# Window attention with a pooled branch: out products in turns, full v spread by DMAs, later batches loaded in pieces

## What is computed

```python
qkv = jnp.einsum('nchw,oc->nohw', xw, qkv_w)            # xw: windows of the normalised x
pooled = _avg_pool5(qkv)
msq = jnp.concatenate([qkv, pooled], axis=1)
msq = msq.reshape(N, -1, 3 * DIM, ws * ws).transpose(0, 1, 3, 2)
q = jax.nn.relu(msq[..., :DIM])
k = jax.nn.relu(msq[..., DIM:2 * DIM])
v = msq[..., 2 * DIM:]
v = jnp.pad(v, ((0, 0), (0, 0), (0, 0), (0, 1)), constant_values=1.0)
kv = jnp.einsum('ngld,nglm->ngdm', k, v)
out = jnp.einsum('ngld,ngdm->nglm', q, kv)
out = out[..., :-1] / (out[..., -1:] + 1e-15)
...
y = jnp.einsum('nchw,oc->nohw', out, proj_w)
y = y * inv[None, :, None, None] + (bn_beta - bn_mean * inv)[None, :, None, None]
return x + y
```

## Time and profile before

| | |
|---|---|
| time, median of three runs | 924.52 us (922.64 to 924.81) |
| the profiled execution's own time | 923.39 us |
| its span | 921.6 us |
| TensorE matmul busy | 862.7 us (94%) |
| TensorE weight load busy | 724.5 us (79%) |
| VectorE busy | 768.1 us (83%) |
| ScalarE busy | 608.1 us (66%) |
| GpSimd busy | 455.0 us (49%) |
| masked pooled v, 576 passes | 224.9 us |
| masked full v, 384 passes | 191.9 us |
| DMA | 38.77 MB |

### The profile page before, as it was taken

How to read it: one execution, slowest core, us unless ns; L and a number is a source line. 1 busy time by engine, 2 the same in 40 slices (tenths; PEclk the granted TensorE clock), 3 DMA queues, 4 the chain that set the end, 5 groups by cost and what they waited for, 6 DMA issues and landing times.

```text
span 921.6 us, 64898 instructions
## 1 busy us (share of the span) xinstructions
PE 862.7 (94%) x29282; PEld 724.5 (79%) x29282; DVE 768.1 (83%) x1624; ACT 608.1 (66%) x1542; POOL 455.0 (49%) x967
## 2 busy tenths in 40 slices
PE   0699999999999999999999999999999999999997
PEld 0577888888888888888888888888888888888885
DVE  7368898998878898998787989999887878787876
ACT  0456767676666767676767676666767676767673
POOL 1544545555454545454545555454545454545550
PEclk9989999999999999999999999999999999999999
DMA  9910000000000000000000000000000000000000
GB/s 380 432 52 17 26 18 26 17 26 17 26 18 26 18 26 17 26 18 26 26 18 26 18 26 17 26 17 27 17 26 17 26 18 26 22 21 26 18 26 27
DMA packets 15893, 38.77 MB, mean 42 GB/s; under 512 B 1888, under 2 KB 14688, under 8 KB 15456
## 3 DMA queue, kind: packets, MB, share of 16 engines
q1 hardware_dynamic: 15840, 38.26, 10.7%
HBM read 19.38 MB, written 18.87 MB: 42 GB/s over the span
## 4 chain that ended last, share of the span: by engine, by line
PE 42%; ACT 39%; issue 14%; DVE 4%; POOL 1%; DMA 0%; ACTq 0%; DVEq 0%; POOLq 0%
ACT vm_pool L305 20%; ACT vm_full L305 15%; PE ps L536 14%; PE ps L564 10%; PE ps L552 9%; PE ps L553 4%; PE ps L636 4%; ACT k_pool L292 3%; DVE stats L377 1%; PE ps L579 1%; PE ps L546 1%; DVE kvc_full L444 1%; DMA x_all<-x 0%; ACT o_sb L332 0%; DVE kvc_pool L444 0%
## 5 line engine op out<-in xcount | busy, mean ns | idle before, releaser
L255 POOL TENSOR_TENSOR xn<-x_all,mean_t 128x384 f32<-128x384 f32 x96 | 79.3, 826 | 388.5 <-PE ps L553 370.0
L305 ACT ACTIVATE vm_pool<-ps,cst 128x256 f32<-128x256 f32 x576 | 224.9, 543 | 0.4 <-PE ps L546 0.4
L444 DVE TENSOR_TENSOR kvc_full<-ps,cst 128x864 f32<-128x864 f32 x192 | 193.2, 1048 | 7.5 <-PE ps L564 7.5
L444 DVE TENSOR_TENSOR kvc_pool<-ps,cst 128x864 f32<-128x864 f32 x192 | 193.2, 1048 | 0.4 <-PE ps L564 0.4
L305 ACT ACTIVATE vm_full<-ps,cst 128x384 f32<-128x384 f32 x384 | 191.9, 597 | 0.9 <-PE ps L536 0.9
L312 ACT ACTIVATE q_full<-ps 128x384 f32<-128x384 f32 x96 | 47.1, 491 | 202.7 <-PE ps L552 202.7
L536 PE MATMUL ps<-wkv_sb,xn 128*128 128x128 f32 x1152 | 146.0, 277 | 23.5 <-POOL xn L256 23.5
L536 PEld LDWEIGHTS ps<-wkv_sb,xn 128*128 128x128 f32 x1152 | 144.8, 194 | 23.5 <-issue 23.4
L450 DVE SCALAR_TENSOR_TENSOR x_all<-ps,shift,x_all 128x384 f32<-128x384 f32 x96 | 59.3, 618 | 100.0 <-PE ps L642 99.8
L579 PEld LDWEIGHTS ps<-kvc_full,q_full 64*32 64x32 f32 x9216 | 99.7, 105 | 26.8 <-issue 26.6
L579 PE MATMUL ps<-kvc_pool,q_pool 64*32 64x72 f32 x9216 | 116.1, 231 | 1.9 <-issue 1.9
(11 more groups left out here) (65 smaller groups left out, 1255.8 us busy)
## 6 DMA issues: line engine op xcount, KB each, us to landing
out<-x_all SPq DMA_DIRECT2D x96, 192.0 KB, 1.9
x_all<-x SPq DMA_DIRECT2D x3, 4608.0 KB, 32.1
x_all<-x SPq DMA_DIRECT2D x6, 768.0 KB, 8.0
cst<-consts SPq DMA_DIRECT2D x1, 172.0 KB, 10.8
wkv_sb<-wkv SPq DMA_DIRECT2D x1, 128.0 KB, 10.6
o_sb<-proj SPq DMA_DIRECT2D x1, 128.0 KB, 10.1
wq_sb<-wq SPq DMA_DIRECT2D x1, 64.0 KB, 10.3
bn_sb<-bn SPq DMA_DIRECT2D x1, 2.0 KB, 10.1
```

The lines of the kernel that those rows point to most:

```text
L255: link(pool.tensor_tensor(xr, src, mean, ALU.subtract), 1)
L305: last = act.activation(heads[:, :, e, :, 0:D], src, ACT.Copy, scale=col(mask + e))
L444: last = dve.tensor_tensor(kvc[:, g], src.to_broadcast(shape), own, ALU.mult)
```

## The change

Masked full v: ScalarE now copies v once from PSUM to a new buffer (`copy_v`, v_full), right after the relu of k and ahead of the image copies. SyncE waits for that copy (v_copied) and issues four DMAs inside SBUF, each of which moves every fourth partition of v_full to the matching part of vm_full (`spread_v`); the other partitions of vm_full stay zero from a memset. For this the four windows of a group alternate from partition to partition, so GpSimd writes the normalised strip in another order, its multiply is split into four, and the relu of q reads PSUM in another order. The column of ones in v_full comes from a memset.

Out products: full and pooled groups (t, e) alternate in one function. The first wait of the pooled ones (for v to have left bank 3) moves ahead of all of them; out_f is raised by the last full matmul, which is followed by the last pooled group.

Loads: the three later images are loaded two strips at a time, one load in each of the first 12 steps of an image, after the four DMAs of `spread_v`; VectorE waits for each piece before its statistics.

The buffers vm_full and vm_pool have their window index outermost. The description of the change says that the pooled residual stays on VectorE; the diff leaves `residual` as it is.

```diff
@@ buffers and semaphores
+        xd = sb("xd", [SP])
...
-        vm_full = sb("vm_full", [TF, EF, 4, KC])
-        vm_pool = sb("vm_pool", [TP, EP, 4, KC])
+        v_full = sb("v_full", [TF, 4 * KC])
+        vm_full = sb("vm_full", [EF, TF, 4 * KC])
+        vm_pool = sb("vm_pool", [EP, TP, 4 * KC])
@@ sync
-            for b in range(1, B):
-                sp.dma_start(x_all[:, b * HW:(b + 1) * HW], x_v[:, b]).then_inc(loaded_batch[b - 1], 16)
-            for b in range(B):
-                for t in range(SPB):
-
-                    sp.wait_ge(y_done, t + (b * SPB + 1))
-                    sp.dma_start(out_v[:, b, bass.ds(t * SP, SP)],
-                                 x_all[:, bass.ds(t * SP + b * HW, SP)]).then_inc(stored, 16)
+            def load_two(b, t):
+
+                wait(sp, loaded_later, 16 * (((b - 1) * SPB + t) // 2))
+                sp.dma_start(x_all[:, b * HW + t * SP:b * HW + (t + 2) * SP],
+                             x_v[:, b, t * SP:(t + 2) * SP]).then_inc(loaded_later, 16)
+
+            def spread_v(s):
+
+
+                sp.wait_ge(v_copied, s + 1)
+                wait(sp, kv_f, s)
+                for e in range(EF):
+                    rows = slice(e, P, EF)
+                    sp.dma_start(vm_full[rows, e], v_full[rows]).then_inc(vm_f, 16)
...
+            spread_v(0)
+            for s in range(NS):
+                if not is_last(s):
+                    spread_v(s + 1)
+                b, t = divmod(s, SPB)
+                if b + 1 < B and 2 * t < SPB:
+                    load_two(b + 1, 2 * t)
+                if not is_first(s):
+                    store(s - 1)
+            store(NS - 1)
@@ gpsimd
+            pool.memset(vm_full[:], 0.0).then_inc(pads_zero, 1)
+            pool.memset(v_full[:], 1.0).then_inc(pads_zero, 1)
...
-                link(pool.tensor_tensor(xr, src, mean, ALU.subtract), 1)
-                pool.tensor_tensor(xn[:, p], xn[:, p], rstd, ALU.mult).then_inc(xn_ready, 1)
+                link(pool.tensor_tensor(xd[:], x_all[:, s * SP:(s + 1) * SP], mean, ALU.subtract), 1)
+                rows = xd[:].rearrange("p (r g e c) -> p r g e c", r=WS, e=EF, c=WS)
+                for r in range(WS):
+                    last = pool.tensor_tensor(xr[:, r], rows[:, r], rstd, ALU.mult)
+                last.then_inc(xn_ready, 1)
@@ scalar
+            def copy_v(s):
+                act.wait_ge(v_f, s + 1)
+                wait(act, vm_f, 16 * EF * s)
+                act.activation(v_full[:].rearrange("p t (h c) -> p t h c", c=HC)[:, :, :, 0:D],
+                               ps[:, V_F, 0:TF * P].rearrange("p (t h m) -> p t h m", t=TF, m=D),
+                               ACT.Copy).then_inc(v_copied, 1)
...
                 if not is_last(s):
                     relu_k(s + 1)
+                    copy_v(s + 1)
                 if not is_first(s):
                     to_image(s - 1)
                     pooled_out(s - 1)
                 if not is_last(s):
-                    masked_v(s + 1, False)
                     relu_k_pooled(s + 1)
-                    masked_v(s + 1, True)
+                    masked_v_pooled(s + 1)
@@ vector
                 if at is not None:
+                    dve.wait_ge(loaded_later, 16 * (((b - 1) * SPB + at) // 2 + 1))
@@ tensor
-                pe.wait_ge(vm_f, s + 1)
+                pe.wait_ge(km_f, s + 1)
+                pe.wait_ge(vm_f, 16 * EF * (s + 1))
...
                 pe.wait_ge(kvc_p, s + 1)
+                if not is_last(s):
+
+                    pe.wait_ge(v_copied, s + 2)
                 pe.nop(nofuse=True)
-                for t in range(TF):
-                    for e in range(WF):
-                        last = out_tile(False, t, e)
+
+                full = [(t, e) for t in range(TF) for e in range(WF)]
+                pooled = [(t, e) for t in range(TP) for e in range(WP)]
+                for (t, e), (t_p, e_p) in zip(full, pooled):
+                    last = out_tile(False, t, e)
+                    last_p = out_tile(True, t_p, e_p)
                 last.then_inc(out_f, 1)
-
-            def out_products_pooled(s):
-                if not is_last(s):
-
-                    pe.wait_ge(vm_f, s + 2)
-                    pe.nop(nofuse=True)
-                for t in range(TP):
-                    for e in range(WP):
-                        last = out_tile(True, t, e)
-                last.then_inc(out_p, 1)
+                last_p.then_inc(out_p, 1)
```

More of the change, by code:

```diff
@@ L149, in build @@
         loaded_first = [sem(f"loaded_first{i}") for i in range(FOURS)]
[L150 removed]
+        loaded_later = sem("loaded_later")
         dv_setup = sem("dv_setup")
@@ L293, in relu_k_pooled, with masked_v_pooled @@
                                ACT.Relu, scale=1 / 25.0).then_inc(km_p, 1)
[L295 to L306 removed]
+            def copy_v(s):
[4 more added lines that the diff above has]
+                               ACT.Copy).then_inc(v_copied, 1)
+            def masked_v_pooled(s):
+                act.wait_ge(v_p, s + 1)
+                wait(act, kv_p, s)
+                heads = vm_pool[:].rearrange("p e t (h c) -> p e t h c", c=HC)
+                src = ps[:, V_P, 0:TP * P].rearrange("p (t h m) -> p t h m", t=TP, m=D)
+                for e in range(EP):
+                    last = act.activation(heads[:, e, :, :, 0:D], src, ACT.Copy, scale=col(C_VP + e))
+                last.then_inc(vm_p, 1)
             def relu_q(s):
@@ L514, in _ @@
             dve.tensor_scalar(proj_sb, proj_sb, bn_inv[:], None, ALU.mult).then_inc(proj_scaled, 1)
-            for vm, wins, mask in ((vm_full, EF, C_VF), (vm_pool, EP, C_TP)):
-                for e in range(wins):
-                    ones = vm[:, :, e].rearrange("p t i (h c) -> p t (i h) c", c=HC)[:, :, :, D]
-                    last = dve.tensor_copy(ones, col(mask + e).unsqueeze(2).to_broadcast(list(ones.shape)))
+            for e in range(EP):
+                ones = vm_pool[:, e].rearrange("p t (h c) -> p t h c", c=HC)[:, :, :, D]
+                last = dve.tensor_copy(ones, col(C_TP + e).unsqueeze(2).to_broadcast(list(ones.shape)))
             last.then_inc(ones_set, 1)
```

62 lines of the change are left out of this document (25 added, 37 removed).

## The result

| | before | after |
|---|---|---|
| median of the runs | 924.66 us (922.64 to 924.91, 4 runs) | 954.91 us (954.13 to 960.18, 4 runs) |
| ratio to before | | 1.0353, 95% interval 1.0315 to 1.039 |
| span of the profiled execution | 921.6 us | 958.3 us |
| strip, mean from strip 4 to 95 | 9.10 us | 9.43 us |

The change makes the kernel 30 us slower. The forecast was 936.7 us: the direction was right, the size too small by 18 us. The ratio is one of means and takes in two more runs of the changed kernel (960.55 and 956.20 us); the two medians alone give 1.033. The profiled execution of after took 960.18 us, 5.3 us above its own median. The granted clock of that run was 0.991, that of the other three 0.996 to 0.998, and in its trace the clock was halved three times before 78 us and again at 951 us, never in between.

The account below looks back on a forecast made before the run. TensorE, with almost no slack apart from 0.46 us per strip, was taken to bound the kernel. 923.4 + 18.4 (new wait) + 0.8 (last strip) - 5.9 (start) = 936.7 us; the range was 903 to 958.

Parts of the forecast that it names:

- The new wait: In each strip, pooled k-v products wait for VectorE's o_full instead of ScalarE's masked pooled v, starting at 407.02 instead of 406.82.
- The term of the new wait: Pooled k-v products' later start: +0.20 us per strip over strips 3 to 94, +18.4 us in the sum.
- the term of the start: Before the loop: loads in pieces, GpSimd's multiplies and v's first spread together give -5.9 us.
- The gain of freeing ScalarE: TensorE's idle time before pooled k-v products: freeing ScalarE alone can bring at most 0.46 us per strip.
- The pace of the turns: The 192 alternating out products still take 1.99 us, a gain of 0, with bounds of nothing and a quarter.
- The rival of faster turns: Alternating makes TensorE's out products faster: 914 us at 0.25 us per strip, 892 at 0.49; chance 0.20.
- The spread of v: SyncE's four copies land at 405.1, hidden before the full k-v products at 405.61; rival of a late spread, chance 0.14.
- The price for a late landing: Landing of v after 406.3 costs 9 us per 0.1 us: 957 us at 406.5, over 1,000 at 407.
- the gain of the pieces: TensorE's start: 4.1 us of a stall and 2.9 us of half clock go, -7.0 us, bounds 0 and -9.
- GpSimd's term: One multiply split into four costs 0.9 us per strip, hidden in the loop and paid once at the start.
- The term for the first spread of v: At the start, the first spread of v by DMAs costs 0.2 us.
- The last strip: The last strip pays VectorE's late start once, +0.8 us.

Follow-up runs that it names:

- experiment 1: The changed kernel with the turns undone: all full out products first, then all pooled ones; 907.1 us, ratio 0.9821.
- experiment 2: The changed kernel with the out products reordered so that the last full group is the ninth of twelve instead of the eleventh; 926.2 us.
- experiment 3: The changed kernel with pooled groups first in the turns, so that the last full group is the twelfth instead of the eleventh; 974.1 us.
- experiment 10: The kernel before with full and pooled out products taking turns, and the wait for v's masks put in front of them; 1019.3 us.
- experiment 4: The changed kernel with a fifth 54 KB copy into a spare buffer, issued ahead of the four that spread v; 976.5 us.
- experiment 5: The kernel of experiment 1 with one more 54 KB copy per strip behind v's four, for which TensorE never waits; 920.1 us.
- experiment 7: The kernel before with four free 54 KB copies per strip between spare buffers, the store placed behind them on SyncE; 925.0 us.
- experiment 8: The kernel before with four free copies per strip of 4 rows, 7 KB each, the store behind them on SyncE; 924.8 us.
- experiment 9: The kernel before with one free copy of 216 KB per strip in place of four of 54 KB; 923.8 us.
- experiment 11: The kernel of experiment 1 without TensorE's wait for the ReLU of full k before the full k-v products; 901.7 us.
- experiment 13: The kernel of experiment 11 with SyncE waiting for v's four parts and raising one semaphore by one for TensorE; 889.6 us, ratio 0.9659.
- experiment 14: The kernel before with only the later images loaded in pieces of two strips instead of whole at the start; 918.8 us, ratio 0.9941.
- 6: The kernel before with four free 54 KB copies per strip between spare buffers, issued behind the strip's store on SyncE; 924.1 us.

## Why the prediction was right or wrong, point by point

**The new wait: right.** The releaser of the pooled k-v products is VectorE's o_full, ScalarE's mask is out of the way, and the rest of the strip is unchanged. Experiments 1 to 3 show it by moving the last full tile.

**The term of the new wait: mis-sized, and this is most of the miss.** It was +0.20 us per strip; measured are +0.33, which is 12 of the 18 us over 91 strips. The step "o_full ends at 406.97, and the pooled k-v products start at 407.02" failed in three small places. TensorE's answer to VectorE was taken as 0.05 us from the tail; with the experiment of the turns alone it is 0.10 (466.72 to 466.82), and the same in the change. VectorE starts 0.01 us later and takes 0.01 us longer (465.43 to 466.72) than forecast. Together these are the 3.47 of experiment 10 against my 3.40. Then "the out products still take 1.99 us" was wrong: den_full starts at +2.12, not +2.08, with the four copies in flight, so the full results come 0.04 us later. That the copies do this fits experiments 4, 5 and 7 to 9; a share of the new layouts is not excluded. 0.20 + 0.07 + 0.04 is 0.31 in the strip shown; the mean over the loop is 0.02 more, in part through three strips of 9.68 us in which VectorE also computes group statistics. The other 6 us are the term of the start, below.

**The gain of freeing ScalarE: right as a bound.** The most was to be 0.46 us per strip; with the full products first and both instructions of experiments 11 and 13 gone, the median strip goes from 9.09 to 8.72 us, 0.37.

**The pace of the turns: right.** Without a copy in flight 192 alternating products take what the two groups took (den_full at +2.08 against a forecast of +2.07). The rival of faster turns is out.

**The spread of v: in time, the side effect missed.** The issues come 0.59 us apart instead of 0.44, and the last part lands 1.86 us behind the last issue, near the 1.9 that I took: at +1.81, where the forecast had +1.48, 0.5 us ahead of the use at +1.99. ScalarE's copy ended where I had put it, and SyncE began 0.03 us behind it instead of 0.1, which made up little of the issue time. So v was in time with 0.2 us to spare. (The price for a late landing, 957 us at 406.5, does not follow from its own 9 us per 0.1: that gives 955.) A transfer was thus put down as hidden once it landed in time. Its cost lay elsewhere: in the products that run beside it. The last out product starts at +2.06 us instead of +1.98; that is 0.04 us on the release of o_full here, and it is 0.15 us per strip for one more copy where TensorE has nothing to wait for. The Trainium skill, DMA: Bandwidth & Descriptors (Rules for kernel authors), wants such transfers joined. The runs agree: from the first issue to the last landing the four copies take 3.6 us, while the one copy of 216 KB in experiment 9 takes 2.2 us and slows the out products least. A joined spread was not tried in the changed kernel.

**The start: the gain of the pieces right in size, the sum wrong.** The step gave -7.0 for the pieces and -5.9 for the whole start; alone the pieces bring -5.1. In the changed kernel nothing of it is left: of 954.9 - 924.7 = 30.2 us between the medians the loop takes 30.1, and in the profiled run the start is 4.5 us longer than before. GpSimd's term (+0.9) was too large, for TensorE's first products start 0.24 us later (23.69 against 23.45), and the pooled ones 0.37. The term for the first spread of v (+0.2) was far too small. The first query comes 2.5 us later than before (35.81 against 33.31) and 2.1 later than in experiment 14 (33.72). TensorE idles 1.27 us for the first spread:

```profile
31.06 0.49 PE L598 MATMUL ps<-vm_full,k_full 64*32 64x144 f32 x8 [1.27 <-DMA vm_full<-v_full]
...
42.99 1.48 PE L598 MATMUL ps<-vm_full,k_full 64*32 64x144 f32 x48 [1.89 <-issue]
...
54.99 0.26 PE L613 MATMUL ps<-kvc_full,q_full 64*32 64x72 f32 x4 [1.68 <-issue]
```

and the two products of the full query take 1.58 us on the chain instead of 0.84. That is their time at half clock (1.58 us again at 73.65, in the stretch from 70.60 below), and the trace's first record of the full clock is at 36.5 us, against 30.9 before. So the first spread costs its wait and then some 1.5 us more through the clock. Behind that come stalls of 1.89, 1.68, 0.89 and 2.54 us and, in the profiled run, three stretches at half clock. Two stretches of after (PE, PEld, DVE, ACT, POOL busy, PEclk, DMA share, GB/s), for the earlier trace rows:

```profile
43.30:46.70 3.40, 3.40 (x81) 2.38 (x60) 2.19 (x3) 0.00 (x0) 0.00 (x0) 0.50 0.26 97
...
70.60:77.50 6.90, 5.54 (x43) 4.01 (x43) 4.02 (x6) 1.09 (x3) 1.39 (x3) 0.51 0.00 0
```

The first follows the stall of 1.89 us, as the one of before followed 5.36; in the second lies the stall of 2.54 us. Yet experiment 14 has stalls of 1.47 to 2.18 us and keeps the full clock, so how long a stall is does not settle it. I had removed one stall with its half clock and assumed that no other would take its place. How much of this is chance of the code's position stays open: strip 4 comes between 76.5 and 85.8 us in the profiled runs of the kernels made from the change with pieces.

**GpSimd, ScalarE, SyncE, VectorE's residual: right.** The four multiplies take 1.27 us together instead of 0.83, 0.44 us more, half of what I had allowed for, and nothing waits for them in the loop. ScalarE's pooled v is ready before it is wanted, and SyncE's store behind the four copies holds nothing up.

**The last strip:** +0.8 worked out, +2.1 in the profiled run, with half clock in it.

## What to carry to other kernels

When an order of work is changed, work out who is released by its last piece. Here the full results were wanted first, and sharing TensorE fairly between two groups delayed the one that others waited for, at 5% of the time. Take the answer time between engines from a row of the same wait in the loop, not from the tail, since a term of 0.05 us is multiplied by the strips. A transfer that lands in time is not yet free, and in front of a group that waits with an empty queue every separate wait and every computed wait value costs; one combined wait on a small constant step is cheaper.

## What the runs showed of the hardware

- Transfers issued while TensorE works through many small matmuls (64 x 32 weights, 72 columns) can slow these, and not by their bytes: 116.1 us of pooled out products became 123.3 with one copy of 216 KB per strip, 132.5 with four of 7 KB and 136.6 with four of 54 KB, and in the kernel of experiment 1 one more of 54 KB made 122.0 us 136.0. A single matmul keeps its 231 ns; the gaps between them grow. The full k-v products (144 columns) kept their 98 us beside copies of 54 KB (98.9 in 6, 98.0 in 7), but took 116.5 us with those of 7 KB.
- A separate wait, and the arithmetic for a wait value, each cost TensorE about 0.1 us where its queue is empty: the median strip went 8.91, 8.82, 8.72 us with none, one and both of them taken away.
- SyncE takes 0.59 us to issue a copy of 54 KB within SBUF when four follow one another, also one of 7 KB (0.61), and the last copy lands 1.86 us behind the start of its issue; behind 14.2 MB of queued loads the same four landed after 21.5 us.
- A stall of TensorE without a releaser, beside which a 16 KB block of the instruction queue moved, was 5.36 us with the DMA engines full and 1.47 us at the same place without. Stalls of 0.7 to 2.5 us came later in the first passes, at places that differ from kernel to kernel.
- TensorE's first matmul that waited for VectorE started 0.10 us behind the end of VectorE's instruction in the loop (466.72 to 466.82), where a row of the last strip had given 0.05 us.
